# Moving the search comparison of a graph kernel from VectorE to ScalarE, as a sign

## The reference, cut to what matters

```python
src = src[argsort(dst)]; dst = dst[argsort(dst)]           # edges sorted by target
h = relu(layernorm(x))
x = x + relu(relu((h + segment_sum(h[src], dst)) @ W1 + b1) @ W2 + b2)
h = relu(layernorm(x))
K, V, Q = h @ Wk + bk, h @ Wv + bv, relu(h @ Wq + bq)     # 8 heads of 8
hidden = V * hopwise[0]
# three hops: sums over edges of norm * outer(K, V)[row], carried from hop to hop
#   norm = deg^-0.5[row] * deg^-0.5[col] * edge_weight
x = x + (hidden + sum_k hopwise[k + 1] * H_k)
```

## Time and profile before

| | |
|---|---|
| median of 3 runs | 1729.83 us (1729.37 to 1741.05) |
| profiled execution: its time, its span | 1737.73 us, 1735.0 us |
| busy share: TensorE, VectorE, ScalarE, GpSimd | 75%, 86%, 59%, 69% |
| `from_here` L1204, VectorE | 49 times, from 25.8 to 337.9 us |
| search on TensorE, L844 | 392 matmul records, 85.4 us |
| signs of the search on ScalarE, L659 | 196 times, 75.9 us |
| GpSimd at the chain's end | output scatter L565, 10% of the span |

### The profile page before, as it was taken

The page is one execution under the profiler, slowest core; times in us unless marked ns, Lnnn a source line. Parts: engine busy times, 40 slices in busy tenths (PEclk is TensorE's granted clock), DMA queues, the critical chain, the costliest instruction groups (busy, mean ns, idle before and its releaser), DMA issues. The chain is left out here.

```text
span 1735.0 us, 22194 instructions
## 1 busy us (share of the span) xinstructions
PE 1301.4 (75%) x5794; PEld 800.3 (46%) x5794; DVE 1487.6 (86%) x3207; ACT 1017.0 (59%) x2815; POOL 1203.7 (69%) x1185
## 2 busy tenths in 40 slices
PE   3788888878888858777771777776588999777771
PEld 2666666656555534554550333323233444454551
DVE  5999999979999958999997999996456788799991
ACT  4688887858999954554552455553455666333330
POOL 7777766707777517777744777774777777777776
PEclk9799999979999967988895899899799999988886
DMA  5255554425666547999995788886345545466640
GB/s 130 80 115 114 127 123 113 127 70 147 159 170 157 145 93 249 317 320 314 305 313 183 271 308 305 300 307 242 92 124 155 158 135 154 132 177 173 176 138 16
DMA packets 281219, 313.83 MB, mean 181 GB/s; under 512 B 169009, under 2 KB 198569, under 8 KB 268550
## 3 DMA queue, kind: packets, MB, share of 16 engines
q1 hardware_dynamic: 224166, 246.39, 45.8%
q0 software_dynamic: 56928, 66.04, 15.0%
HBM read 214.54 MB, written 161.32 MB: 217 GB/s over the span
## 5 line engine op out<-in xcount | busy, mean ns | idle before, releaser
L946 PE MATMUL bank<-product,ident 128*128 128x512 f32 (+1 forms) x800 | 382.5, 635 | 137.6 <-DVE product L1302 137.5
L549 POOL DMA_INDIRECT state<-state_hop,slot_of_src x392 | 395.2, 1008 | 126.1 <-issue 108.0
L719 ACT ACTIVATE bank<-state,norm 128x512 f32<-128x512 f32 x392 | 251.2, 679 | 254.2 <-DMA state<-state_hop,slot_of_src 218.0
L1302 DVE TENSOR_TENSOR product<-bank,queries 128x512 f32<-128x512 f32 x392 | 261.9, 689 | 91.3 <-ACT bank L719 89.6
L946 PEld LDWEIGHTS bank<-product,ident 128*128 128x128 f32 x800 | 160.6, 206 | 357.7 <-issue 183.7
L511 POOL DMA_INDIRECT x_edges<-in_x,dst_tiles x196 | 203.5, 1039 | 106.2 <-issue 53.9
L525 POOL DMA_INDIRECT row_of_src<-node_rows,pos_int x196 | 195.3, 996 | 104.1 <-issue 54.3
L511 POOL DMA_INDIRECT x_edges<-in_x,src_tiles x196 | 210.0, 1071 | 75.1 <-issue 55.2
L565 POOL DMA_INDIRECT out<-rows,dst_out x196 | 193.3, 986 | 59.7 <-issue 58.8
L1300 DVE SCALAR_TENSOR_TENSOR acc<-acc,same_as_before,bank 128x512 f32<-128x512 f32 x196 | 145.7, 744 | 15.1 <-ACT bank L719 14.7
L1113 DVE SCALAR_TENSOR_TENSOR acc<-acc,same_as_before,bank 128x512 f32<-128x512 f32 x196 | 145.8, 744 | 1.7
(11 more groups left out here) (220 smaller groups left out, 2992.1 us busy)
## 6 DMA issues: line engine op xcount, KB each, us to landing
state_hop<-acc SPq DMA_DIRECT2D x98, 1024.0 KB, 4.6
x_nodes<-in_x SPq DMA_DIRECT2D x49, 256.0 KB, 4.2
src_row<-in_src_row SPq DMA_DIRECT2D x49, 256.0 KB, 3.9
out<-out_rows SPq DMA_DIRECT2D x49, 256.0 KB
dst_row<-in_dst_row SPq DMA_DIRECT2D x49, 256.0 KB, 3.4
kv_rows<-kv SPq DMA_DIRECT2D x49, 256.0 KB, 3.1
gg<-head_sums SPq DMA_DIRECT2D x98, 128.0 KB
kv_back<-kv_rows SPq DMA_DIRECT2D x49, 256.0 KB
```

The costliest lines, as they stand in the source:

```text
L549: pool.indirect_dma_start(out=mg[u % 4][:, k, :], out_offset=None, in_=d_m[hop - 1], in_offset=bass.IndirectOffsetOnAxis(ap=sidx[:, t:t + ...
L719: act.activation(pw[t % len(pw)][:, :], mg[u % 4][:, k, :], ACT.Copy, scale=wn12[:, t:t + 1]).then_inc(weighted, 1)
L946: ins = ten.matmul(ph[:, 0:k * D].rearrange("p (c j) -> p c j", j=HD), ident[:, :], part, start=(r == 0), stop=(r == HD - 1))
L1302: vec.tensor_tensor(ihj(pr[m % 2][:, u % 2 * EH + k, :]), ihj(pw[t % len(pw)][:, :]), over_j(Q[:, t, :]), ALU.mult).then_inc(multiplied, 1)
```

## The change

The comparison is taken from VectorE's list and put, as a sign, into ScalarE's, in the same tick, behind the Square of the edge rows. `sign(src - dpm[:, 0] + 0.5)` is 1 where the comparison gave 1, and -1 where it gave 0. To make the same sums from it, the steps `delta` are halved, and half of their total is put in by the first partition: `dprev[0]` is now loaded with the last partition's targets and negated, so that partition 0's step is its own targets plus the last ones, and the 197th column holds T / 2 (first partition: T + 127 T / 2). The bias of the sign is a new column `rowb`. There is one more load (15 for 14) and three more small VectorE instructions, and one memset turns into another. The selection comparisons (`select`) stay where they are.

```diff
@@ SyncE
             for to, what in ((dpm[:, :], dst_pm), (dprev[1:P, :], dst_pm[0:P - 1, :]),
+                             (dprev[0:1, :], dst_pm[P - 1:P, :]),
@@ ScalarE, behind the Square of the edge rows
+                u = g - 1
+                if 0 <= u < CU:
+                    if u == 0:
+                        act.wait_ge(consts_set, 1)
+                    act.wait_ge(srow_in[u % 3], landed(u, u % 3, 3))
+                    wait(act, searched, u - 1)
+                    act.activation(gsel[u % 2][:, :], srow[u % 3][:, :], ACT.Sign, bias=rowb[:, 0:1]).then_inc(g_set, 1)
@@ VectorE, constants
-            own.add(vec.memset(dprev[0:1, :], 0.0))
-            own.add(vec.memset(delta[:, T:T + 1], float(T)))
+            step(vec.memset(delta[:, T:T + 1], T / 2))
+            own.add(vec.memset(delta[0:1, T:T + 1], T + (P - 1) * T / 2))
             own.sync()
             vec.wait_ge(cleared, 1)
             vec.wait_ge(loaded, 16 * N_LOADS)
+            step(vec.tensor_scalar(dprev[0:1, :], dprev[0:1, :], -1.0, None, ALU.mult))
             step(vec.tensor_tensor(delta[:, 0:T], dpm[:, :], dprev[:, :], ALU.subtract))
+            own.add(vec.tensor_scalar(delta[:, 0:T], delta[:, 0:T], 0.5, None, ALU.mult))
+            own.add(vec.tensor_scalar(rowb[:, :], dpm[:, 0:1], -1.0, 0.5, ALU.mult, ALU.add))
@@ VectorE, end of the tick
-                u = g - 1
-                if 0 <= u < CU:
-                    vec.wait_ge(srow_in[u % 3], landed(u, u % 3, 3))
-                    wait(vec, searched, u - 1)
-                    vec.tensor_scalar(gsel[u % 2][:, :], srow[u % 3][:, :], dpm[:, 0:1], None, ALU.is_ge).then_inc(g_set, 1)
```

More of the change, by code:

```diff
@@ L198, in gnn @@
         st = [sb(f"stats{b}", [P, 6, COLS]) for b in range(RS)]
+        rowb = sb("row_begins", [P, 1])
         epsc, warm = sb("eps_col", [P, 1]), sb("root_of_one", [P, 1])
@@ L333, in gnn @@
         block = ctx.enter_context(nc.Block())
-        N_LOADS = 14
+        N_LOADS = 15
         def dense_rows(t, m):
```

## The result

| | before | after |
|---|---|---|
| median of 4 runs each, same chip | 1734.05 us (1729.37 to 1741.05) | 1755.46 us (1749.96 to 1757.67) |
| profiled execution: time, span | 1737.73, 1735.0 us | 1753.93, 1751.9 us |
| VectorE busy, share of the span | 86% | 84% |
| search on TensorE, busy | 85.4 us (L844) | 95.3 us (L853) |

The ratio is 1.0115, with a 95% interval of 1.0066 to 1.0164: the change makes the kernel about 1.2% slower, some 20 us by the ratio. My likeliest case was 13.3 us more (0.8%). Where a ratio further down is called plain, it is that of the mean times, with the runs of each kernel left out that lie over 1.5% above its fastest.

A forecast was written before the change was run, and what follows sets the result against it. The bound was taken as a round trip between VectorE's variance and ScalarE's root, with `from_here` hidden in it. 1.1 + 3.2 + 3.5 + 6.3 - 0.8 = 13.3 us more gave a median of 1743 us, range 1731 to 1754.

The forecast's parts named there:

- likeliest case: Whole kernel: the later comparison costs 13.3 us, median 1743 us; chance 0.5 for its own range, 1737 to 1749.
- The shadow: VectorE, between variance and reciprocal: `from_here` fills the wait for ScalarE's root, so removing its 0.48 us returns nothing.
- Rival 1: VectorE, node stage: VectorE is the bound and is relieved, 23.5 us less, 1706 us; chance 0.05.
- Longer `from_here`s, -0.8: VectorE: only the part of 43 comparisons above 0.48 us can come back, 0.8 us less, bounds 0 and 1.5.
- The Sign on ScalarE, cost 0: ScalarE, 49 ticks: the added Signs are barely hidden in its idle time before the root, cost 0.
- Rival 4: ScalarE becomes the bound with a Sign of 1.04 us start to start: 8 us on top, 1751 us; chance 0.07.
- The stores, +6.3: SyncE's list: row stores behind the later comparison land late and VectorE waits, 6.3 us more, bounds 0 and 11.
- The first ticks, +3.2: From 26 to 50 us: Sign and Squares enter the loop of root and search, 3.2 us more, bounds 1.5 and 5.
- The stretches of half clock, +3.5: TensorE, three half-clock stretches: its later start lengthens VectorE's wait for the root, 3.5 us more, bounds 0 and 6.
- Setup, +1.1: Before the ticks: one more SyncE load and three more VectorE instructions, 1.1 us more, bounds 0.6 and 1.5.
- rival 3: Stores' wait at its upper end plus a fourth half-clock stretch: 20.5 us more, 1750 us; chance 0.2.
- my 0.68 for a change within 1%: Whole kernel: chance 0.68 that the time stays within 1% (17 us), which a measurement can't tell from no change.

The follow-up runs named there:

- the store first: Changed kernel with the load of the next sources moved behind the row store in SyncE's list: 1740.64 us, ratio 1.0021 to the kernel before.
- the two best versions: Changed kernel, store first, Sign behind root, first five comparisons on VectorE: 0.9866. Kernel before, store first, `out_rows` and `x_nodes` blocks ahead of the reciprocal: 0.9945 and 0.9852.

## Why the prediction came out as it did

*The shadow: right, with one thing missing.* The reciprocal starts 0.56 us after the variance in both kernels, but for the ten long variances of after (0.74 to 0.79), which nothing in my sum foresaw and which cost 2.1 us. It waits for the root in 48 ticks, 30.1 us in all (in two of them the rows name no releaser); without the waits of the first four ticks (3.62 + 2.21 + 2.83 + 3.35 = 12.0) that is 18.1, a little over the 15 I named. Rival 1 failed on the chip as well: without any comparison the kernel gains 0.5%, not 1.3%.

*Longer `from_here`s, -0.8: not seen.* Three ticks without a store's wait take 18.63 us after (309.51 to 328.14, with one slow search in them) and 18.52 before: nothing comes back there, and 0.1 is lost for which no row gives a cause.

*The Sign on ScalarE, cost 0: nearly.* I took 0.52 us start to start from the Square; it is 0.61. The smallest slack had been 0.66, so it is eaten to 0.05 in one tick of three. ScalarE waits for the variance in 42 ticks, 0.9 us a time (37.8 / 42), not the 0.5 I named; the mean hides that in a dozen ticks it doesn't wait at all. Where the root followed its variance after 0.21 us even so, this cost nothing. Rival 4 (a Sign over 0.88) did not come.

*The stores, +6.3: right mechanism, and near in size.* SyncE's issues and VectorE's waits, after:

```profile
244.68 0.56 SPq L445 DMA_DIRECT2D out<-out_rows  x1
249.70 0.69 DVE L1166 TENSOR_TENSOR out_rows<-bank,x_nodes 128x512 f32<-128x512 f32 x1 [0.58 <-DMA out<-out_rows]
250.86 0.57 SPq L445 DMA_DIRECT2D out<-out_rows  x1
257.35 0.69 DVE L1166 TENSOR_TENSOR out_rows<-bank,x_nodes 128x512 f32<-128x512 f32 x1 [1.82 <-DMA out<-out_rows]
```

The store at 244.68 is issued 3.11 us after the root at 241.57; I had 3.01 (231.38 - 228.37). It was taken as landed 5.0 us later, and the next, at 250.86, 6.5 later, where I had 4.6 for both. So the waits grew from 6.0 to 13.5 us, 7.5 more. Fifteen waits fall in two kinds: eight of under 0.6, 0.42 on average (3.4 us), as worked out (0.37), and seven of 0.7 to 2.9 (10.1 us), where the store took up to 6.5. The Trainium skill, page "DMA: Bandwidth & Descriptors", section "Anatomy of one DMA", fits a DMA issued by GpSimd by about 2.0 us plus its bytes over 436 GB/s, which gives an estimate of 2.6 us for this size. The runs disagree with it for stores from SyncE's list (5.0 and 6.5 us), as the loads of the earlier trace rows did.

*The first ticks, +3.2 (3.6 up to tick 6): the step that failed.* 6.8 us were measured at tick 6. The chain root, Squares, Sign, search was right: the roots of ticks 2 and 3 come 1.4 and 3.0 later, where 1.2 and 2.6 were worked out. What was wrong is, for ticks 3 and 4, "ScalarE is simply full, 0.5 each": I kept the search at 1.60 us there, as the trace of before had it, but the third and fourth search took 2.99 and 2.83. The third ran ahead of the clock's first full-speed entry, which comes at 43.5 us after the change and came at 35.4 us before it; the fourth ran at a granted clock of 0.54. The pauses ahead of them, in which TensorE waited for the late comparison, are 1.20 and 1.44 us, against 0.55 and 0.54 before. The slow searches are 1.4 + 1.2 = 2.6 us of the 3.2 missing, and the first two ticks 0.4. The reciprocal of 45.41 came at

```profile
51.63 0.28 DVE L1155 RECIPROCAL stats<-stats 128x20 f32<-128x20 f32 x1 [3.35 <-ACT stats L668]
```

6.2 us later, where I had named 4 to 5.

*The stretches of half clock, +3.5: the slow searches came, their price did not.* I carried over the three stretches of before and made each a bit longer. Instead there were twelve slow searches after the first four, scattered, all but one behind pauses of 1.4 to 4.1 us, and they cost VectorE's chain little each. Waits for a late root, beyond the usual 0.38 us, are 1.4 us in ticks 10 to 53 (at 276.41, 335.19 and 354.73), and they were 1.4 before (at 127.98 and 282.73), so they did not grow at all; new are 0.7 us of waits of `x_nodes` for TensorE's product. By the sum of the terms, 6.8 - 1.3 + 7.5 + 2.1 + 0.7 and 0.5 behind the stage, some 16.3 of the 16.9 us are named.

*Setup, +1.1: wrong, 0.* The first root is at 25.88 us in both. VectorE's constants start at 14.64 and not at 14.83, and the three instructions made nothing later. In the other traces of kernels with the same setup it varies by about a microsecond (25.8 to 27.1), so a term of this size can't be read from one execution.

*Not in the sum:* 1.3 us back in the preparations of ticks 6 to 9, of which I had 0.4.

So the terms were 3.2, 6.3, 3.5, 1.1 and -0.8; they measured as 5.5 (6.8 less 1.3), 7.5, 0.7, 0 and nothing seen, and 2.1 us of long variances had no term. The likeliest case held in its mechanism. That its sum of 13.3 comes near the 16.9 of the profiled executions is in part luck: 3.9 us too much for the half clock and the setup stand against 3.5 too little for the first ticks and the stores. By the ratio the change costs some 20 us, which is the number of rival 3 (20.5) but not its reason, for the stores' wait did not reach the 11 us that it had, nor the half clock the 6. Of the ratio, 1.0115, the interval begins inside 1% and ends at 1.6%: my 0.68 for a change within 1% was too much and the 0.27 for slower too little, and the largest reason is the first ticks' term, which I costed with the searches of the trace before.

What stays open: why the changed kernel is not slower on the slower chip, where the time lies outside the ticks that it touches; what makes a quarter of the variances twice as long; what the store first is worth in the kernel before; and what the two best versions take on the first chip.

## What to carry to other kernels

A busy engine is not relieved by taking away what it does while it would wait anyway: look at what starts behind the instruction, and whether its input is ready when the instruction goes. When an instruction moves to another engine, its duration is the smaller part; list what is queued behind its result (here an in-order DMA list, and through it the stores of another stage), and move those ahead, which was worth 0.9% to the changed kernel. TensorE's durations in a trace belong to the pauses in front of it: here 16 of 49 searches were slow after the pauses had grown, and 5 before. Where a change lengthens them, cost the matmuls behind at the slower duration as well. And before a granted clock of 1.00 is read as full speed, see that the trace has an entry there.

## What the runs showed of the hardware

With a column as bias ScalarE's instruction was longer. Sign of 128x512 from SBUF to SBUF without one took 615 ns (mean of 43; the Square of that shape takes 0.61 us); with a column as bias it took

```profile
L687 ACT ACTIVATE from_here<-src_row,row_begins x49: 704/707/750, 26.9 to 354.9; 128x512 f32<-128x512 f32 x49
```

(least, median and most, ns), 0.09 more, and as much more from start to start. The two read different buffers, so that the column is the cause is the nearest reading and not shown by itself.

The first searches take 2.96 to 3.00 us, as at 1.2 GHz. In the fourteen traces 24 searches that show as one row end before the clock's first entry, and each of them took that long; the views show 1.00 there for want of an entry. From the first entry on, the record and the durations agree, and some searches are slow for a part only (2.07 to 2.92 us). The first full-speed entry comes behind the second search in the kernel before and behind the third in the changed one.

Chips differ by 20% in this kernel: 1737 us on one, 2077 on two others, with a mean granted clock of 0.89 against 0.79 to 0.82, and stretches near the start in which TensorE, VectorE and ScalarE stand still together. The loss of 1.15% measured on the first did not show on the one other chip where the changed kernel ran.
